# Eight of 64 states of a selective scan: inflow by GpSimd, decay in PSUM

## The reference, cut to what matters

```
delta = softplus(dt @ dt_w.T + dt_b)
h = h * exp(delta[d] * A[d, s]) + (delta * xc)[d] * B[t, s]
y[d] += h[d, s] * C[t, s]
```

## Time and profile before

| | us |
|---|---|
| median of three runs | 611.45 |
| profiled execution, its own time | 610.64 |
| its span, first to last instruction | 608.9 |
| TensorE busy | 503.9 (83%) |
| VectorE busy | 467.1 (77%) |
| ScalarE busy | 442.7 (73%) |
| GpSimd busy | 331.7 (54%) |

### The profile page before, as it was taken

The page is one execution under the profiler, slowest core; times in us unless marked ns, Lnnn a source line. Parts: engine busy times, 40 slices in busy tenths (PEclk is TensorE's granted clock), DMA queues, the critical chain, the costliest instruction groups (busy, mean ns, idle before and its releaser), DMA issues.

```text
span 608.9 us, 9243 instructions
## 1 busy us (share of the span) xinstructions
PE 503.9 (83%) x3378; PEld 415.4 (68%) x3378; DVE 467.1 (77%) x709; ACT 442.7 (73%) x845; POOL 331.7 (54%) x155
## 2 busy tenths in 40 slices
PE   3569979969899996989988969698776666989997
PEld 3246757759687685878855858697665554788696
DVE  5857799769887785898899859989999997484032
ACT  2469868999997799999867899889797710443060
POOL 3105648769875686796657759667586651100000
PEclk9898999998999999799999889799899899685999
DMA  7030222212322212132221202212452240000101
GB/s 251 0 108 36 70 69 71 89 52 76 101 80 95 71 70 69 67 110 71 72 69 43 94 38 93 86 70 70 137 174 71 70 138 1 0 2 2 34 1 36
DMA packets 17885, 43.46 MB, mean 71 GB/s; under 512 B 1328, under 2 KB 7600, under 8 KB 17584
## 3 DMA queue, kind: packets, MB, share of 16 engines
q1 hardware_dynamic: 17840, 42.87, 21.4%
HBM read 41.56 MB, written 1.31 MB: 70 GB/s over the span
## 4 chain that ended last, share of the span: by engine, by line
PE 39%; ACT 27%; DVE 25%; issue 6%; POOL 2%; DMA 1%; DVEq 0%; ACTq 0%; POOLq 0%
ACT dBuT L572 12%; DVE area L975 10%; PE yT L1190 9%; PE pro L1190 9%; PE yT L1194 8%; ACT dA L565 7%; PE dBu L1194 6%; PE dBu L1190 5%; DVE area L971 3%; POOL hc L481 2%; PE pro L1194 2%; DVE area L763 1%; ACT th L533 1%; ACT pre L540 1%; ACT area L555 1%
## 5 line engine op out<-in xcount | busy, mean ns | idle before, releaser
L481 POOL TENSOR_TENSOR hc<-area 128x1024 f32<-128x1024 f32 x127 | 304.0, 2396 | 157.8 <-DVE area L971 90.9
L572 ACT ACTIVATE dBuT<-area,bT 128x256 f32<-128x256 f32 x508 | 215.1, 498 | 13.8 <-PE dBu L1194 13.8
L1194 PE MATMUL dBu<-ident,dBuT 128*128 128x128 f32 x1024 | 149.3, 284 | 42.5 <-DVE area L975 23.2
L565 ACT ACTIVATE dA<-area,Aneg 128x1024 f32<-128x1024 f32 x128 | 146.2, 1143 | 20.4 <-DVE area L975 13.5
L1194 PEld LDWEIGHTS dBu<-ident,dBuT 128*128 128x128 f32 x1024 | 119.7, 145 | 56.8 <-issue 22.2
L1194 PE MATMUL yT<-ident,hc 128*128 128x128 f32 x1024 | 140.6, 283 | 1.7 <-POOL hc L481 1.4
L1194 PEld LDWEIGHTS yT<-ident,hc 128*128 128x128 f32 x1024 | 120.9, 145 | 20.0 <-issue 16.0
L975 DVE TENSOR_TENSOR_SCAN area<-dA,area,dBu 128x512 f32<-128x512 f32 x64 | 81.8, 1278 | 4.6
L971 DVE TENSOR_TENSOR_SCAN area<-dA,area,dBu 128x512 f32<-128x512 f32 x64 | 81.8, 1278 | 4.2
L971 DVE TENSOR_TENSOR_SCAN area<-dA,dBu 128x512 f32<-128x512 f32 x64 | 77.2, 1206 | 7.9 <-PE dBu L1194 7.5
L975 DVE TENSOR_TENSOR_SCAN area<-dA,dBu 128x512 f32<-128x512 f32 x64 | 77.1, 1205 | 6.6 <-PE dBu L1194 6.0
(11 more groups left out here) (226 smaller groups left out, 577.0 us busy)
## 6 DMA issues: line engine op xcount, KB each, us to landing
area<-c_rows SPq DMA_DIRECT2D x64, 512.0 KB, 3.6
dBuT<-w_in SPq DMA_DIRECT2D x1, 2048.0 KB, 9.0
wp<-wpack_in SPq DMA_DIRECT2D x1, 1030.0 KB, 7.3
x<-x_in SPq DMA_DIRECT2D x2, 512.0 KB, 6.5
hc<-bcast_in SPq DMA_DIRECT2D x1, 1024.0 KB, 10.2
out<-x SPq DMA_DIRECT2D x4, 256.0 KB, 2.3
hT<-w_in SPq DMA_DIRECT2D x1, 512.0 KB, 7.3
acc<-w_in SPq DMA_DIRECT2D x1, 512.0 KB, 7.1
```

The costliest lines, as they stand in the source:

```text
L481: g_.tensor_tensor(hc[:, e % 3, :], hs[:, e % 3, :], Cb[:, g % 3, :], ALU.mult).then_inc(hc_done, 1)
L565: nc.scalar.activation(dA[:, e % 3, :], delta[par][:, half, :], ACT.Exp, scale=Aneg[:, dr, half, s:s + 1]).then_inc(da_ready, 1)
L572: return nc.scalar.activation(dBuT[:, g % 2, n, :], duT[par][:, n, :], ACT.Copy, scale=bT[:, par, n, s:s + 1])
L1194: return nc.tensor.matmul(out, in_, ident[:, :] if idn is None else idn, start=start, stop=True, is_transpose=True, skip_group_check=True)
```

## The change

For eight states (unit 0: 4, 7; units 1 and 2: 1, 4, 7; so tiles 8, 9, 14, 15, 34, 35, 40, 41, 46, 47, 66, 67, 72, 73, 78, 79) the two operands of the scan change places. SP spreads the row of B too (`Bb`, one buffer; `crow_d` now holds B and C). GpSimd multiplies du by it straight into the tile's dA buffer, both halves one after the other, ahead of the hc of the state before. ScalarE writes the decay in two pieces of 512 into the dBu banks that the turns would have filled. The scalings and the turns of these states go. `du` moves from yg to `pre`. The counts of semaphores follow.

```diff
+DIRECT = [DS * u + s for u, s in [(0, 4), (0, 7), (1, 1), (1, 4), (1, 7), (2, 1), (2, 4), (2, 7)]]
+SCALED = [g for g in range(NG) if g not in DIRECT]
...
-        du = yg
+        du = pre
+        Bb = sb("Bb", [P, L])
...
-                    sp.dma_start(crow_d[u], xdbl[DR + DS:XD, :]).then_inc(c_stored, 16)
+                    sp.dma_start(crow_d[u], xdbl[DR:XD, :]).then_inc(c_stored, 16)
...
+                if g + 1 in DIRECT:
+                    k = DIRECT.index(g + 1)
+                    if k:
+                        sp.wait_ge(direct_ready, NH * k)
+                    sp.dma_start(Bb[:, :], crow_d[u, s + 1:s + 2, :].partition_broadcast(P)).then_inc(bb_ready, 16)
...
+            def direct_product(e):
+
+                k, half = DIRECT.index(e // NH), e % NH
+                g_.wait_ge(bb_ready, 16 * (k + 1))
+                g_.wait_ge(du_ready, NH * (e // (DS * NH)) + half + 1)
+                g_.wait_ge(scan_done, NCH * (e - 2))
+                g_.tensor_tensor(dA[:, e % 3, :], du[:, half, :], Bb[:, :], ALU.mult).then_inc(direct_ready, 1)
...
+                if e % NH == 0 and e // NH + 1 in DIRECT:
+                    direct_product(e + NH)
+                    direct_product(e + NH + 1)
                 g_.wait_ge(scan_done, NCH * (e + 1))
...
+            def exp_chunk(e, i):
+
+                u, s, half = e // (DS * NH), e // NH % DS, e % NH
+                _, dr, par = unit(u)
+                q, c = NCH * e + i, chunks(u)[i]
+                act.wait_ge(scan_done, q - 2)
+                nc.scalar.activation(dBu[q % 3][:, :], delta[par][:, half, c * CH:(c + 1) * CH], ACT.Exp,
+                                     scale=Aneg[:, dr, half, s:s + 1]).then_inc(da_ready, 1)
...
-                if e + 1 < NT:
+                direct = (e + 1) // NH in DIRECT
+                if direct:
+                    exp_chunk(e + 1, 0)
+                elif e + 1 < NT:
                     exp_tile(e + 1)
                 first = g + 1 < NG and (g + 1) % DS == 0
                 if half == 0:
-                    if g + 1 < NG:
+                    if g + 1 < NG and g + 1 not in DIRECT:
                         scale_blocks(g + 1, 0 if first else 1)
                 else:
                     if first:
                         scale_blocks(g + 1, 1)
-                    if g + 2 < NG and (g + 2) % DS != 0:
+                    if g + 2 < NG and (g + 2) % DS != 0 and g + 2 not in DIRECT:
                         scale_blocks(g + 2, 0)
+                if direct:
+                    exp_chunk(e + 1, 1)
                 if e and ENDS[e - 1] is not None:
                     item_a(*ENDS[e - 1])
...
+                decay, inflow = dA[:, e % 3, lo:hi], dBu[q % 3][:, :]
+                if direct:
+                    decay, inflow = inflow, decay
...
-                    if e + 1 < NT:
+                    if e + 1 < NT and (e + 1) // NH not in DIRECT:
                         dbu_chunk(e + 1, i)
```

More of the change, by code:

```diff
@@ L109, in count_of, with directs, dbu_count, da_count @@
     return sum(o[0] in kinds for o in ORDER[:NUMBER[it] + 1])
+def directs(e):
+    return sum(NH * g < e for g in DIRECT) * NH - (e // NH in DIRECT and e % NH == 1)
+def dbu_count(e, i):
+    return NCH * (e - directs(e)) + i + 1
+def da_count(e, i):
+    return e + directs(e) + i + 1
 def product_at(e):
@@ L247, in build_block @@
         da_ready = sem("da_ready")
+        bb_ready = sem("b_row_ready")
+        direct_ready = sem("direct_dbu_ready")
         dbut_ready = sem("dbut_ready")
@@ L539, in item_a @@
                     dst, func = (delta[par], ACT.Softplus) if u == 0 else (pre, ACT.Identity)
+                    if u > 0:
+                        act.wait_ge(direct_ready, NH * sum(g < DS * u for g in DIRECT))
                     nc.scalar.activation(dst[:, half, c * CH:(c + 1) * CH], src, func,
@@ L583, in scale_blocks @@
                     wait_item(act, "BT", 0, u)
-                if g >= 2:
-                    freed = list(chunks((g - 2) // DS)).index(c)
-                    act.wait_ge(dbu_ready, NCH * (NH * (g - 1) - 1) + freed + 1)
+                if SCALED.index(g) >= 2:
+                    old = SCALED[SCALED.index(g) - 2]
+                    freed = list(chunks(old // DS)).index(c)
+                    act.wait_ge(dbu_ready, dbu_count(NH * old + 1, freed))
                 for n in range(c * BPC, (c + 1) * BPC):
@@ L960, in scan_chunk @@
                 c = chunks(u)[i]
[L961 to L965, removed]
+                direct = e // NH in DIRECT
+                if i == 0 and e >= 3:
+                    dve.wait_ge(hc_done, e - 2)
+                if direct:
+                    if i == 0:
+                        dve.wait_ge(direct_ready, NH * DIRECT.index(e // NH) + e % NH + 1)
+                    dve.wait_ge(da_ready, da_count(e, i))
+                else:
+                    if i == 0:
+                        dve.wait_ge(da_ready, da_count(e, 0))
+                    dve.wait_ge(dbu_ready, dbu_count(e, i))
                 if i:
@@ L968, in scan_chunk @@
                 lo, hi = c * CH, (c + 1) * CH
+                decay, inflow = dA[:, e % 3, lo:hi], dBu[q % 3][:, :]
+                if direct:
+                    decay, inflow = inflow, decay
                 if u % 2 == 0:
                     init = hs[:, e % 3, lo - 1:lo] if i else 0.0
-                    nc.vector.tensor_tensor_scan(hs[:, e % 3, lo:hi], dA[:, e % 3, lo:hi], dBu[q % 3][:, :],
-                                                 init, ALU.mult, ALU.add).then_inc(scan_done, 1)
+                    nc.vector.tensor_tensor_scan(hs[:, e % 3, lo:hi], decay, inflow, init, ALU.mult, ALU.add).then_inc(scan_done, 1)
                 else:
                     init = hs[:, e % 3, hi:hi + 1] if i else 0.0
-                    nc.vector.tensor_tensor_scan(hs[:, e % 3, lo:hi][:, ::-1], dA[:, e % 3, lo:hi][:, ::-1],
-                                                 dBu[q % 3][:, ::-1], init, ALU.mult, ALU.add).then_inc(scan_done, 1)
+                    nc.vector.tensor_tensor_scan(hs[:, e % 3, lo:hi][:, ::-1], decay[:, ::-1], inflow[:, ::-1], init, ALU.mult, ALU.add).then_inc(scan_done, 1)
             def gate(u, half):
```

14 lines of the change are left out of this document (7 added, 7 removed).

## The result

The changed kernel takes 623.22 us (median of 4 runs, 622.57 to 624.50) against 611.22 us (4 runs, 610.56 to 612.16) on the same chip: a ratio of 1.0198, 95% interval 1.0176 to 1.0220, so 12.0 us slower. The direction is the forecast's, the size is not: 616.2 was expected, and 621 was the upper end. The profiled execution took 624.5 us, its span is 622.8 us (before 608.9), TensorE's mean granted clock 0.910 (before 0.933).

A forecast was written before the change was run, and what follows sets the result against it. No single engine was taken as the bound, which changes from slot to slot. Held items and gains +1.3 us and clock falls +3.4 make +4.7: 615.3 profiled, 616.2 us on the median's scale; range 607 to 621 (own 613.5 to 619.5).

The forecast's parts named there:

- What is removed: TensorE loses 13.9 us of turns, ScalarE 25.6 of scalings; gains -2.4 us (unit 1 state 4), -1.4 (unit 2 state 4).
- I cost them at nothing: GpSimd's 16 added products (38.3 us) and SP's transfers of B's row: covered by waiting time and slack, 0 us.
- The wait that comes with it: ScalarE's item of a pair's second tile stands behind exponential pieces waiting for scans: +0.3, +1.6, +0.8 twice, +0.2, +1.4 us.
- TensorE's clock: In both state 1 pairs TensorE idles 3.6 us and falls to half clock: +3.4 us for two (0 to 2.6 each).
- ScalarE does not hold the items: In a pair's second tile ScalarE finishes its pieces before TensorE hands over; only gains remain, 607.6 us; chance 0.22.
- the clock stays: No fall of TensorE's clock in the state 1 pairs; only +1.3 us remains, 612.8 us; chance 0.20.
- GpSimd becomes the bound: Products and hc hold a pair by up to 4.8 us, nearest in unit 0 state 7; 618.6 us; chance 0.11.

The follow-up runs named there:

- run 8: Kernel before with the change for state 4 of units 1 and 2 only, ScalarE's scalings kept, writing to a spare buffer: 605.22 us, ratio 0.9900.
- run 2: Kernel before with GpSimd's 16 products and SP's transfers of B's row added, the products unread: 616.10 us, ratio 1.0066.
- Run 1: Changed kernel without GpSimd's 16 products and the waits on them: 619.79 us, ratio 1.0115 against the kernel before.
- run 3: Changed kernel with ScalarE's item right behind the first exponential piece, ahead of scalings and second piece: 615.10 us, ratio 1.0056 against the kernel before.
- run 4: Changed kernel with 16 identity turns on TensorE at the start of the third slot of units 1 and 2: 617.72 us, ratio 1.0083 against the kernel before.

## Why the prediction was off

The steps, in its own order:

- **What is removed** (the turns) was right in place and size: -2.4 us in unit 1 state 4. In unit 2 state 4 the O items gave 1.6 us (forecast 1.4); the other 1.2 of the 2.8 is the wait missed in tile 73. One cause stays half open: the 0.68 us of unit 1 were put down to copies that come earlier by ScalarE's freed 1.60 us. It is not that freed time, as the 0.68 us go with the scalings kept, but run 8 drops the scalings' wait on TensorE too.
- **"I cost them at nothing", the products: the step that failed.** The prediction asks who waits for GpSimd through semaphores, and finds nobody; that part is true (run 2). But VectorE's TENSOR_SCALARs, and operations with both operands in SBUF, waited for the end of a GpSimd instruction with no semaphore between them. Term: 0 forecast; measured +0.4, +2.7 and +1.9 us met and -1.2 missed, +3.8 net. Run 1, without the products, was 3.4 us faster; run 2, with nothing but them, 3.8 us slower. The sign was in the trace of before: a TENSOR_SCALAR of 128x8 that lasts 1.89 us. (The two 3.8 agree in part by chance: run 2 met other such waits, and other falls of the clock.)
- **The wait that comes with it**, ScalarE's hold: right. Terms +0.3, +1.6, +0.8, +0.8, +0.2 and +1.4, 5.1 us; measured +0.5 (0.9, less 0.4 of tile 9's wait), +1.6, +0.8, +0.8, +0.9 and +1.4, 6.0 us. The one that missed is unit 1 state 7: I let a freed turn win back 0.35 us, which did not come, and the tanh starts 0.35 us later than the sum has it (210.68 for 210.33), since the second piece of tile 46 is still running on ScalarE when the first of tile 47 could start. Putting the item first took the hold away (run 3).
- **TensorE's clock**: the two falls forecast came, after gaps of 3.61 and 3.62 us, and cost 1.3 to 2.8 and 1.5 to 1.6 us (1.7 each forecast). So did one in unit 2 state 7, after 3.11 us, and it cost nothing there, as forecast. But the step read a rule off two gaps of one execution (3.11 no, 3.44 yes). The other executions refute it: 3.10 us with a fall, and gaps of 2.04 us in tile 47 with one (first execution) and without (run 4); that the two came is no proof of the rule. And by the rule itself tile 11 was missed: the prediction reads the gap of 3.11 us and does not ask what the change does to it. It grows to 3.74, and +1.7 us come with it in all three executions (the kernel before has that fall in one of three).
- **After the scan** nothing was forecast. The changed kernel takes 3.3 to 3.9 us longer there than the first execution of the kernel before, though no instruction differs. Over all fourteen traces the stretch takes 114.9 to 115.0 us in seven, with TensorE's clock at half of full speed for 34 us of it, and 117.4 to 118.9 in the other seven, with 40 to 44 us at half. The five with all eight states and the item behind the pieces (the changed kernel, runs 1 and 4) are all of the longer kind, but so are two of the nine others, a kernel before among them. How much of it the change brings stays open.

Sum for the first execution: 4.7 forecast, +3.8 for the products, +3.1 for falls not foreseen (tiles 11, 12 and 47), +3.9 after the scan, -1.6 in tiles 81 to 83; that is 13.9, as much as lies between the spans (smaller rows cancel). The medians are only 12.0 us apart: the profiled execution of before lies 0.6 us under its median, that of the changed kernel 1.3 us over.

Of the rivals, "ScalarE does not hold the items" is refuted by the tables, "the clock stays" by the view by stretch, and "GpSimd becomes the bound" by run 2 in the form that it had, hc late behind the products. GpSimd did cost time, by another way.

## What to carry to other kernels

A free engine is not free work: before costing an operation on GpSimd at nothing, look in VectorE's groups for operations whose longest is some 2 us above their median, and count how many of them the new work will meet. A queue's order can cost more than its work: the item ahead of the same scalings and second piece, instead of behind them, gave 5 to 6 us of the scan back. And a change to several places is better judged place by place: in the changed kernel two of the eight pairs held the whole gain, and those two alone are 0.9% faster than the kernel before.

## What the runs showed of the hardware

- A VectorE TENSOR_SCALAR in SBUF that comes up while a GpSimd instruction runs lasts until that one is over: 336 ns becomes up to 2394 ns; three of eight met one in the changed kernel, one of eight before. A TENSOR_TENSOR with both operands in SBUF behaves alike (1.20 and 3.05 us). The scan, with one operand in PSUM, does not (1.28 us). GpSimd waits in its turn: in the kernel before, the hc that starts at 322.71, while a TENSOR_TENSOR of 1.20 us runs on VectorE, takes 3.28 us in place of 2.36.
- An exponential of 128x512 into PSUM took 0.68 us on ScalarE, and two in a row 1.28 us together; the forecast's 0.71 and 0.61, worked out from shapes written to SBUF, are near both. The Trainium skill, "ScalarE: Activation LUTs", section on the step-by-step, has writes to PSUM as the faster ones; by it the forecast would have put the piece at 0.50 us. The row, 0.03 us under the 0.71, agrees in direction and by no more than that.
- The length of an idle gap alone doesn't tell whether TensorE's clock goes to half of full speed: 3.10 and 3.11 us before the same instruction of the same kernel, and the X behind it took 3.08 us in the one execution and 1.98 in the other. A fall in tiles 35, 47 and 67 cost 1.3 to 2.8 us, and 16 turns of an unused block in the gap avoided those behind tiles 34 and 66.
- The same kernel's executions differ by up to 5 us (609.8 to 614.7 over 18 runs of before), and most of what the traces show of it is where the clock falls.
